# Collecting the experts' outputs inside the state layer's block, in four chunks of 512 tokens

## The reference, cut to what matters

```
x = x + gate[:, 0] * y_of_first_expert + gate[:, 1] * y_of_second_expert      # end of layer 2
n = layernorm(x)                                                              # layer 3, state layer
conv = conv_b + sum(n_padded[k : k + L] * conv_w[k] for k in range(4))
proj = conv @ Wp + bp
B_t, C_t, u = softplus(proj[:, :64]), tanh(proj[:, 64:]), n @ Ws + bs
decay = 1 - softplus(dt_log) * softplus(A_log)
state_t = decay * state_(t-1) + softplus(dt_log) * B_t * u_t                  # over all 2048 tokens in order
x = x + (C_t * state_t) @ Wo + bo
```

## Time and profile before

| | us |
|---|---|
| median of 3 runs | 3772.86 (3768.91 to 3777.5) |
| the profiled execution | 3772.7 |
| its span, first to last instruction | 3771.0 |
| last store of expert output issued | 3555.42 |
| collection, VectorE's last multiply-add ends | 3601.14 |
| state layer, VectorE's last add ends | 3659.14 |

### The profile page before, as it was taken

The page is one execution under the profiler, slowest core; times in us unless marked ns, Lnnn a source line. Parts: engine busy times, 40 slices in busy tenths (PEclk is TensorE's granted clock), DMA queues, the critical chain, the costliest instruction groups (busy, mean ns, idle before and its releaser), DMA issues. The chain is left out here.

```text
span 3771.0 us, 127464 instructions
## 1 busy us (share of the span) xinstructions
PE 3189.7 (85%) x54136; PEld 2083.8 (55%) x54136; DVE 2905.2 (77%) x3610; ACT 2530.5 (67%) x4874; POOL 640.9 (17%) x1650
## 2 busy tenths in 40 slices
PE   2999999749999799477586499999999999999538
PEld 1666666425555577123445266666666666666324
DVE  5999999548886211699457499999999999999553
ACT  1899999627778343443223089999999999999522
POOL 0000000023211000199000011111111111111210
PEclk7899999869999899688788599999999999999759
DMA  5000000040000000252029745555555555545310
GB/s 122 7 10 8 10 8 8 8 110 14 10 9 3 18 17 11 89 195 78 6 65 251 190 104 130 125 119 134 118 132 125 128 127 120 138 120 130 94 28 12
DMA packets 190765, 295.12 MB, mean 78 GB/s; under 512 B 87922, under 2 KB 119994, under 8 KB 189142
## 3 DMA queue, kind: packets, MB, share of 16 engines
q1 hardware_dynamic: 185238, 275.64, 28.8%
q10 hardware_dynamic: 2608, 6.37, 0.8%
q0 software_dynamic: 2352, 4.99, 0.5%
HBM read 224.83 MB, written 53.35 MB: 74 GB/s over the span
## 5 line engine op out<-in xcount | busy, mean ns | idle before, releaser
L889 ACT ACTIVATE channels_qk<-psum 128x512 f32<-128x512 f32 x3842 | 2060.5, 595 | 259.5 <-PE psum L718 224.3
L957 DVE TENSOR_REDUCE l2f_chunk_max<-psum 128x2 f32<-128x1024 f32 x1144 | 1323.6, 1218 | 80.9 <-PE psum L694 74.4
L957 DVE TENSOR_REDUCE chunk_max<-psum 128x2 f32<-128x1024 f32 (+2 forms) x832 | 916.4, 1158 | 100.8 <-PE psum L694 59.3
L694 PE MATMUL psum<-l2f_k_parts,l2f_q_parts 48*128 48x512 bf16 x2288 | 697.8, 388 | 42.3 <-DVE l2f_chunk_max L957 31.2
L736 PE MATMUL psum<-channels_qk,l2f_v_and_ones 128*9 128x128 f32 x17920 | 700.4, 275 | 13.2 <-issue 13.2
L718 PE MATMUL psum<-l2f_q_parts,l2f_k_parts 51*128 51x128 bf16 x8968 | 706.8, 218 | 1.3 <-issue 1.3
L694 PE MATMUL psum<-k_parts,q_parts 48*128 48x512 bf16 (+3 forms) x1664 | 427.4, 383 | 102.0 <-DMA q_parts<-q_rows_dram 70.1
L718 PEld LDWEIGHTS psum<-l2f_q_parts,l2f_k_parts 51*128 51x128 bf16 x8968 | 482.9, 94 | 31.5 <-ACT channels_qk L889 25.1
L736 PE MATMUL psum<-channels_qk,v_and_ones 128*9 128x128 f32 x12544 | 494.4, 276 | 1.7 <-ACT channels_qk L889 0.9
L718 PE MATMUL psum<-q_parts,k_parts 51*128 51x128 bf16 x6272 | 433.2, 219 | 33.0 <-DMA q_parts<-minus_max_rows 12.4
L736 PEld LDWEIGHTS psum<-channels_qk,l2f_v_and_ones 128*9 128x9 f32 x17920 | 387.3, 90 | 120.4 <-issue 25.0
(11 more groups left out here) (494 smaller groups left out, 3109.3 us busy)
## 6 DMA issues: line engine op xcount, KB each, us to landing
l2f_k_parts<-l2f_k_parts_dram SPq DMA_DIRECT2D x588, 192.0 KB, 3.9
l2f_v_and_ones<-expert_v_dram SPq DMA_DIRECT2D x144, 288.0 KB
l1a_bc_rows<-ssm_rows_dram SPq DMA_DIRECT2D x32, 512.0 KB, 4.7
expert_v_dram<-l2f_v_and_ones SPq DMA_DIRECT2D x8, 1152.0 KB, 9.9
channels_qk<-ssm_rows_dram SPq DMA_DIRECT2D x16, 512.0 KB
l2f_q_parts<-l2f_gathered_q_parts SPq DMA_DIRECT2D x444, 16.0 KB
k_parts<-k_rows_dram ACTq DMA_DIRECT2D x32, 192.0 KB, 6.2
q_parts<-q_rows_dram SPq DMA_DIRECT2D x64, 96.0 KB, 2.5
```

The source lines that it names most:

```text
L694: last = nc.tensor.matmul(c.ps[:, 2 * (n % 2) + j, 0:width], at.q[64 * j:64 * j + ROWS, tile % SLOTS, pair, :], kx(tile)[64 * j:64 * j + R ...
L889: nc.scalar.activation(at.prob[:, s % 4, j, 0:kts, :].rearrange("p k q -> p (k q)"), c.ps[:, ring.bank(i, n), 0:kts * 2 * P], ACT.Exp, sca ...
L957: v.tensor_reduce(at.mx[:, 4 * g + 2 * pp:4 * g + 2 * pp + 2, chunk], c.ps[:, 2 * (n % 2):2 * (n % 2) + 2, 0:span.width(tile, chunk)], X, ...
```

## The change

`l2_collect` and its block go. `gate` and `y_row` are allocated outside the attention's memory, so that they outlive it, and `end_sublayer` now stands between the attention loop and the merged block. In that block:

- SyncE issues the ten weight loads at once, beside GpSimd's 32 gathers, which are the same as before.
- VectorE first does `steps()` (the decay of the recurrence, which needs the small softplus and so the weights), then four chunks of 512 tokens. For each: `collect(k)` with the statistics of each tile behind its two multiply-adds, `add(k - 2)`, `normalise(k)`, `states(k - 1)`, `convolve(k)` with the bias row at its end. `states(3)`, `add(2)` and `add(3)` end it. The scan of a chunk starts from the last column of the one before.
- TensorE for each chunk: four transposes, the projection `u`, two projections `p`, then the output projection of the chunk before. A chunk uses one half of the PSUM banks, by turns; chunk k waits for `add(k - 2)`.
- ScalarE for each chunk: square root, copy of the transposed tiles, `u` with bias, Abs, Exp, Ln, Tanh. The small softplus stands first.

The diff, cut to its core; GpSimd, TensorE, ScalarE and VectorE follow in this order (semaphore names and allocations are left out):

```diff
-def l2_collect(c, rt, gate, y_row):
...
+            @block.gpsimd
+            def _(pool):
+                for t in range(NT):
+                    for k in range(2):
+                        nc.gpsimd.indirect_dma_start(out=y[k][:, t, :], out_offset=None, in_=y_dram.rearrange("i p d -> (i p) d"),
+                                                     in_offset=bass.IndirectOffsetOnAxis(ap=y_row[:, k, t:t + 1], axis=0)).then_inc(gathered[t // B], 16)
...
+                for k in range(NC):
+                    pe.wait_ge(n_ready, k + 1)
+                    if k >= 2:
+                        pe.wait_ge(y_added, k - 1)
+                    for t in range(TILES):
+                        last = nc.tensor.transpose(bank(k, 0)[:, t * P:(t + 1) * P], c.n[:, TILES * k + t, :], c.ident[:, :])
+                    last.then_inc(nT_psum, 1)
...
+                    nc.tensor.matmul(bank(k, 1)[0:N, :], ws[:, :], xp[:, KC - 1 + k * 512:KC - 1 + (k + 1) * 512], start=True, stop=True).then_inc(u_psum, 1)
+                    pe.wait_ge(conv_ready, k + 1)
+                    for part in range(2):
+                        nc.tensor.matmul(bank(k, 2 + part)[0:N, :], wp[:, part * N:(part + 1) * N], conv[:, columns(k)],
+                                         start=True, stop=True).then_inc(p_psum, 1)
+                    if k:
+                        out(k - 1)
+                out(NC - 1)
...
+                act.wait_ge(w_loaded, 16 * len(loads))
                 softplus_scalar(c, act, link, log[:, :], 0.0, sp_[:, :], tl[:, :]).then_inc(dt_ready, 1)
+                for k in range(NC):
+                    act.wait_ge(var_ready, k + 1)
+                    nc.scalar.activation(c.std[:, tiles(k)], c.var[:, tiles(k)], ACT.Sqrt).then_inc(std_ready, 1)
+                    act.wait_ge(nT_psum, k + 1)
+                    nc.scalar.activation(xp[:, KC - 1 + k * 512:KC - 1 + (k + 1) * 512], bank(k, 0), ACT.Copy).then_inc(nT_ready, 1)
+                    act.wait_ge(u_psum, k + 1)
+                    nc.scalar.activation(u[:, columns(k)], bank(k, 1)[0:N, :], ACT.Identity, bias=bs[:, :]).then_inc(u_ready, 1)
+                    act.wait_ge(p_psum, 2 * k + 1)
+                    softplus_scalar(c, act, link, bank(k, 2)[0:N, :], bp[:, 0:1], mag[:, columns(k)], b_t[:, columns(k)]).then_inc(tail_ready, 1)
+                    act.wait_ge(p_psum, 2 * k + 2)
+                    nc.scalar.activation(c_t[:, columns(k)], bank(k, 3)[0:N, :], ACT.Tanh, bias=bp[:, 1:2]).then_inc(c_ready, 1)
...
+                def collect(k):
+                    for t in range(TILES * k, TILES * k + TILES):
+                        dve.wait_ge(gathered[t // B], 16 * 2 * B)
+                        for n in range(2):
+                            link(v.scalar_tensor_tensor(c.x[:, t, :], y[n][:, t, :], gate[:, n, t:t + 1], c.x[:, t, :], ALU.mult, ALU.add))
+                        last = v.bn_stats(c.moments[:, t, :], c.x[:, t, :])
+                    link(last)
+
+                def normalise(k):
+                    for t in range(TILES * k, TILES * k + TILES):
+                        last = v.bn_aggr(c.mean_var[:, t, :], c.moments[:, t, :])
+                    link(last)
+                    v.tensor_scalar(c.var[:, tiles(k)], c.mean_var[:, tiles(k), 1], 1e-5, None, ALU.add).then_inc(var_ready, 1)
+                    dve.wait_ge(std_ready, k + 1)
+                    link(v.reciprocal(c.rstd[:, tiles(k)], c.std[:, tiles(k)]))
...
+                def states(k):
+                    now = columns(k)
+                    dve.wait_ge(tail_ready, k + 1)
...
+                    link(v.tensor_tensor_scan(b_t[:, now], decay[:, :].to_broadcast([N, 512]), u[:, now],
+                                              b_t[:, k * 512 - 1:k * 512] if k else 0.0, ALU.mult, ALU.add))
+                    dve.wait_ge(c_ready, k + 1)
+                    v.tensor_tensor(c_t[:, now], c_t[:, now], b_t[:, now], ALU.mult).then_inc(y_ready, 1)
...
+                link(v.memset(xp[:, 0:KC - 1], 0.0))
+                steps()
+                for k in range(NC):
+                    collect(k)
+                    if k >= 2:
+                        add(k - 2)
+                    normalise(k)
+                    if k >= 1:
+                        states(k - 1)
+                    convolve(k)
+                states(NC - 1)
+                add(NC - 2)
+                add(NC - 1)
```

More of the change, by code:

```diff
@@ L2551, in _, with l3_state @@
                 keys_lo(7)
-def l2_collect(c, rt, gate, y_row):
[L2556 to L2578, removed]
+def l3_state(c, ins, gate, y_row, y_dram):
     nc = c.nc
@@ L2609, in _ @@
             @block.tensor
             def _(pe):
-                norm.tensor(pe)
-                pe.wait_ge(w_loaded, 16 * len(loads))
-                pe.wait_ge(norm.nT_ready, NC)
-                for k in range(NC):
[L2615 to L2623, removed]
-                    last.then_inc(p_psum, 1)
@@ L2644, in _ @@
                 link = Chain(dve, chain)
-                link(v.memset(xp[:, 0:KC - 1], 0.0))
-                norm.vector(dve, link)
-                dve.wait_ge(w_loaded, 16 * len(loads))
-                dve.wait_ge(norm.nT_ready, NC)
-                link(v.tensor_scalar(conv[:, :], xp[:, 0:T], conv_w[:, 0:1], conv_b[:, :], ALU.mult, ALU.add))
-                for k in range(1, KC):
-                    last = v.scalar_tensor_tensor(conv[:, :], xp[:, k:k + T], conv_w[:, k:k + 1], conv[:, :], ALU.mult, ALU.add)
-                    if k < KC - 1:
-                        link(last)
@@ new lines, in normalise @@
+                def normalise(k):
[5 more added lines that the diff above has]
+                    link(v.reciprocal(c.rstd[:, tiles(k)], c.std[:, tiles(k)]))
+                    for t in range(TILES * k, TILES * k + TILES):
+                        last = v.tensor_scalar(c.n[:, t, :], c.x[:, t, :], c.mean_var[:, t, 0:1], c.rstd[:, t:t + 1], ALU.subtract, ALU.mult)
+                    last.then_inc(n_ready, 1)
+                    dve.wait_ge(n_ready, k + 1)
@@ new lines, in convolve @@
+                def convolve(k):
+                    dve.wait_ge(w_loaded, 16 * len(loads))
+                    dve.wait_ge(nT_ready, k + 1)
+                    link(v.tensor_scalar(conv[:, columns(k)], xp[:, k * 512:(k + 1) * 512], conv_w[:, 0:1], conv_b[:, :], ALU.mult, ALU.add))
+                    for n in range(1, KC):
+                        last = v.scalar_tensor_tensor(conv[:, columns(k)], xp[:, n + k * 512:n + (k + 1) * 512], conv_w[:, n:n + 1], conv[:, columns(k)],
+                                                      ALU.mult, ALU.add)
+                        if n < KC - 1:
+                            link(last)
+                    last.then_inc(conv_ready, 1)
+                    link(v.tensor_tensor(c.x[:, tiles(k), :], c.x[:, tiles(k), :], b_out[:, :].unsqueeze(1).to_broadcast([P, TILES, P]), ALU.add))
```

82 lines of the change are left out of this document (44 added, 38 removed).

## The result

| | before | after |
|---|---|---|
| median of 16 runs, us | 3770.78 (3757.23 to 3779.93) | 3762.09 (3753.31 to 3767.97) |
| the profiled execution | 3772.7 | 3757.58 |
| its span | 3771.0 | 3755.8 |
| last store of expert output issued | 3555.42 | 3551.16 |
| state layer, VectorE's last add ends | 3659.14 | 3646.37 |

The ratio is 0.9975, with a 95% interval of 0.9966 to 0.9984: 0.25% faster, 8.7 us, with an interval of 6.0 to 12.8. The prediction said 9.5.

A forecast was written before the change was run, and what follows sets the result against it. Collection was bound by issuing gathers (one every 1.25 us), the state layer by a chain across three engines. After block start 22.0 + 3 x 18.46 + 13.5 = 90.9 us, 9.5 less than before: 3763.4 us, range 3757 to 3770.

The forecast's parts named there:

- tail: From the last chunk's convolution to VectorE's last add: ScalarE's functions, states, output matmuls and add, 13.5 us.
- the stretch: From the issue of the last expert store to the end of VectorE's last add; forecast 9.5 us shorter.
- The boundary: Last expert store to merged block: store lands after 1.6 us, then semaphore clearing and barrier, 1.67.
- The head: Merged block's start to the end of chunk 0's convolution: weights, `steps()`, collecting, normalising, convolving; 22.0 us.
- The period: From one chunk's finished convolution to the next's, a turn through TensorE, ScalarE and VectorE: 18.46 us.
- What is hidden: All gathers, and some 7 us of VectorE's bias, collecting, add and aggregates, lie under TensorE's and ScalarE's 10 us.
- The table loads: ScalarE in the merged block: 17 loads, 1.28 us each, four per period; no Exp load at the start.
- That it does not pay: Rival: weights 2 us late and dearer hand-overs (3) take half the gain; about 3768.4 us, chance 0.23.
- GpSimd excluded beside VectorE: Rival: gathers cannot issue while VectorE works in the merged block; 9.2 us slower, 3782, chance 0.05.
- Drains at a change of table: Rival, on ScalarE's changes of function: one of the two slower cases, chance 0.02.
- VectorE's pace: Rival: if functions shared tables, each chunk would take VectorE's own 14.9 us; gain 20, 3753 us, chance 0.04.
- TensorE at full clock: Rival: first projection costs 1.1 us and output 1.2, so 4.6 less; 3758.8 us, chance 0.08.

The follow-up runs named there:

- the swap: Changed kernel with ScalarE's square root of chunk k+1 ahead of chunk k's Tanh; median 3751.90 us of 4 runs, ratio to before 0.9954.
- the chunks-alone kernel: Changed kernel, but the collection keeps a block of its own and the state layer works by four chunks behind it; 3807.65 us (one run).
- the kernel without loads: Changed kernel with Copy, Abs or Identity for Sqrt, Exp, Ln and Tanh in the four chunks; last store to last add 95.56 us, run again 81.04.

## Why the prediction was right

By its own steps, in us; the five rows behind the first are all counted from the block's start:

| step | predicted | measured |
|---|---|---|
| store issued to block start | 3.28 | 3.08 |
| to the end of the weights' wait | 8.7 | 8.8 |
| to the start of `steps()` | 10.7 | 10.9 |
| to the end of collecting chunk 0 | 15.3 | 15.4 |
| to the end of its normalising | 17.4 | 17.6 |
| to its convolution's end | 22.0 | 22.5 |
| three periods | 55.4 | 55.8 |
| tail | 13.5 | 13.8 |
| the stretch | 94.2 | 95.2 |
| less than before's 103.7 | 9.5 | 8.5 |

**The boundary** and **the loads** came out to 0.2. That a boundary without `end_sublayer` is cheaper is in the trace of before: from VectorE's last add of the state layer (3659.14) to its next instruction (3659.68) are 0.54, and from its last multiply-add (3601.14), with `end_sublayer` between, to its next (3602.99) 1.85. The first gather started 0.69 after the block's start, not 0.3, and nothing waited for it.

**The head** was 0.5 long. 0.2 was there when chunk 0 was normalised, and came from the loads and the small softplus; 0.3 came with the turn and the convolution, 0.1 of it from the first convolution step, which takes 0.55 and not the 0.43 of the earlier trace rows, a row of another tensor of the same size.

**The period** was 0.1 to 0.2 long in each. Its largest part, ScalarE's 8.03, holds: from Abs at 3578.77 to the end of the square root at 3586.84 are 8.07. TensorE's part of the sum, 2.05, is an estimate that no run shows by itself: one pass at twice the 3.37 / 8 of the row at a granted clock of 1.00, one of 1.12, and hand-overs. In after the granted clock over each pair was 0.50, a pass took 0.92 (3.68 / 4), and from the convolution's end to the start of Abs are 2.06 (3595.27 to 3597.33). The scan, priced from half of a row at 1024 columns at 1.27, took 1.22 in chunk 0 and 1.28 in the others, whose start value lies in memory. That 64 partitions cost as much as 128 is right: 0.74 for the multiply by B_t (line 2693) against 0.75 of the earlier trace rows.

**What is hidden** is right as a whole: the chunks-alone kernel and the one with a quarter of the gathers have the same periods within 0.01. VectorE's idle time before the reciprocals was forecast at 3 to 4 us; it was 4.95, 3.90 and 3.15. The first, outside the forecast, is longer since chunk 1 has no `add` before it. The add's own wait was 0.48 and 1.23 (1 in the prediction).

**The table loads** are as counted, 17 in the block, with no Exp load in the head, and none showed more than its 1.28. Here the prediction stopped one step short: it took four loads in a period as given and did not ask whether another order of the four functions has fewer. The swap shows that it can have three, and that Tanh need not stand on the path at all.

**Rivals.** That it does not pay, about 3768.4, did not come: the loads were 0.1 late, not 2, and the steps behind them were dearer by 1 us in all, not 3. *GpSimd excluded beside VectorE*: seven gathers took 1.05 to 1.68 and the whole issuing some 2 us more. The prediction had named a gather over 1.5 us as a sign that it is wrong, and one of the 32 gave that sign. In the kernel that merges without chunks none took over 0.98, so the longer gathers came with what the chunks put beside them; which instruction does it no run isolates. It cost nothing: the last gather was issued at 3595.6, the chunk that needed it was collected from 3614.5 on, and by the kernel with a quarter of the gathers VectorE lost nothing to them. (In this rival's sum 23 x 1.25 is 28.75, not 28.6.) *Drains at a change of table*, a chance of 0.02 and one of the two slower cases: no run shows any. From the end of Abs to the start of Exp are 1.31 us, of which 1.28 are the load, in before (3630.74 to 3632.05) as in after. *VectorE's pace* did not come in after, but it is what follows once the loads are gone. It was given a gain of 20; the kernel without loads gained 103.72 - 81.04 = 22.7. Against after it is 11.3 less in the periods, where the rival had 10.5, and 2.6 in the tail, which loses two loads as well (11.23 instead of 13.80). Its argument, that every one of these changes of function shows a load, did not hold for Tanh to Exp. *TensorE at full clock* did not come by itself: all four projections ran at a granted clock of 0.50, and so did the last output, which took 2.07 (2.0 in the prediction).

**The total** agrees for the right reason: 8.5 by the stretch against 9.5 by the sum, the missing 1.0 spread over head (0.5), periods (0.4) and tail (0.3), less 0.2 at the boundary. That the median moved by 8.7 is closer to the sum than its own interval (6.0 to 12.8) can vouch for.

## What to carry to other kernels

A stage that is paced by issuing transfers can carry the first part of the next stage's chain, even one that was made longer for it: here chunks alone lose 32 us, and gain 5 once they lie under the gathers. When a chunked loop turns round an engine, write down that engine's work in order and put last what no one waits for; on ScalarE this also decides how many table loads there are (three in a chunk instead of four in the swap). And judge a change of some us in a program of 3.8 ms by a stretch between two events around it, since the program ahead moved by 11 us from execution to execution.

## What the runs showed of the hardware

- Exp behind Tanh shows no table load, with Copy, Identity and Abs between (3594.32 to 3594.36 in the swap), and behind a square root one of 1.28 us (1.31 from Abs to Exp in after). That is one load fewer in each of chunks 1 to 3.
- Seven of GpSimd's 32 indirect DMAs took 1.05 to 1.68 us beside the chunks' steps, where before none took more than 1.07 and with the collection merged alone none more than 0.98; the median hardly moved (0.943 to 0.947 us).
- In after, all four pairs of projections, each behind an idle time of 1.0 to 3.3 us, ran at a granted clock of 0.50 and took 3.67 to 3.68 us. Right behind chunk 1's pair the clock was 0.86 for 1.4 us. With spare matmuls in the gap the pairs took 1.93 to 1.95, at a granted clock of 0.98 to 1.00. Spare work costs where it ends behind its data: 14 matmuls ahead of the first projections made them start 3.3 us later than in after, and four made them start 0.9 later, about what they gave back.
- In one execution VectorE stood idle for 14.7 us in a stretch of 18, with no cause in the profile, and ScalarE and TensorE started late as well, while the gathers kept their pace; the same kernel did not show this again.
